# Bias of the values and of the feed-forward output folded into other biases during setup; the first graph's x loaded ahead of the weights

## The reference, cut to what matters

```
q = x @ Wq + bq;  k = x @ Wk + bk          (8 heads of 32)
attn = softmax(q k^T / sqrt(32))
out  = sum over r of (attn * (adj == r)) @ (x @ Wv[r] + bv[r])
x1 = ln(x + out @ Wo + bo) * g1 + beta1
x2 = ln(x1 + gelu(x1 @ W1 + b1) @ W2 + b2) * g2 + beta2
```

## Time and profile before

| | |
|---|---|
| median of 3 runs | 3253.69 us (3249.42 to 3253.93) |
| the profiled execution, its own time | 3253.88 us |
| its span, from first to last instruction | 3252.1 us |
| mean granted clock of TensorE | 0.99 |
| PE busy | 3119.1 us (96%) |
| PE's weight loads, beside the matmuls | 2711.1 us (83%) |
| DVE busy | 2710.2 us (83%) |
| ACT busy | 2063.7 us (63%) |
| POOL busy | 1473.1 us (45%) |

### The profile page before, as it was taken

One profiled execution on the slowest core, in us unless ns is written; L12 is line 12 of the kernel. 1 busy time (PEld: TensorE's weight loads), 2 busy tenths in 40 slices (PEclk: granted clock), 3 DMA queues, 4 the chain that ended last, 5 costly groups with the idle time before them and its releaser, 6 DMA issues.

```text
span 3252.1 us, 77634 instructions
## 1 busy us (share of the span) xinstructions
PE 3119.1 (96%) x28930; PEld 2711.1 (83%) x28930; DVE 2710.2 (83%) x4892; ACT 2063.7 (63%) x4300; POOL 1473.1 (45%) x1549
## 2 busy tenths in 40 slices
PE   3999999999999999999999999999999999999996
PEld 2788888888888888888888888888888888888885
DVE  3688888888888888888888888888888888888884
ACT  2566766766766666666666666666666666666664
POOL 1345345345355355355455454454454454454441
PEclk8999999999999999999999999999999999999997
DMA  4333433433433433433433433433433433433431
GB/s 107 82 80 93 104 78 92 105 78 91 107 78 90 107 78 89 108 78 88 109 78 87 109 79 87 108 79 87 105 82 87 104 84 87 103 85 87 101 84 30
DMA packets 217643, 292.63 MB, mean 90 GB/s; under 512 B 31492, under 2 KB 119048, under 8 KB 217608
## 3 DMA queue, kind: packets, MB, share of 16 engines
q1 hardware_dynamic: 217608, 292.16, 38.0%
HBM read 72.89 MB, written 16.78 MB: 28 GB/s over the span
## 4 chain that ended last, share of the span: by engine, by line
PE 81%; DVE 14%; issue 2%; SPq 1%; DMA 1%; ACT 1%; POOL 0%; DVEq 0%; ACTq 0%; POOLq 0%
PE pair L922 44%; PE pair L952 11%; PE pair L976 7%; DVE n L686 5%; PE pair L1035 4%; PE pair L967 4%; PE pair L968 4%; PE pair L940 3%; PE pair L1044 2%; PE pair L927 2%; DVE n L680 2%; DVE n L744 1%; DVE x2t_lo L659 1%; DVE stats L671 1%; SPq L309 1%
## 5 line engine op out<-in xcount | busy, mean ns | idle before, releaser
L396 POOL TENSOR_TENSOR act_r_lo<-act,act_r_hi 128x512 fp32r<-128x512 f32 x256 | 334.8, 1315 | 748.7 <-DVE act_r_hi L886 550.3
L502 ACT ACTIVATE leaky_s<-leaky_s,low_r 128x256 f32<-128x256 f32 x1024 | 505.9, 498 | 2.9 <-DVE low_r L728 2.1
L523 ACT ACTIVATE probs<-pair 128x1024 f32<-128x1024 f32 x256 | 256.7, 1029 | 202.0 <-PE pair L1044 202.0
L402 POOL TENSOR_TENSOR probs<-probs,rel 128x512 f32<-128x512 f32 x256 | 327.2, 1300 | 124.7 <-ACT probs L523 124.7
L732 DVE TENSOR_REDUCE mx_a<-pair 128x4 f32<-128x1024 f32 x256 | 308.0, 1224 | 80.2 <-PE pair L1035 79.9
L496 ACT ACTIVATE leaky_s<-pair 128x1024 f32<-128x1024 f32 x256 | 261.9, 1023 | 159.3 <-PE pair L968 159.3
L724 DVE TENSOR_TENSOR leaky_s<-pair,leaky_s 128x1024 f32<-128x1024 f32 x256 | 312.1, 1219 | 28.5 <-ACT leaky_s L496 28.3
L728 DVE TENSOR_REDUCE low_r<-leaky_s 128x4 f32<-128x1024 f32 x256 | 310.5, 1213 | 2.2
L492 ACT ACTIVATE probs<-pair 128x1024 f32<-128x1024 f32 x256 | 261.8, 1023 | 63.7 <-PE pair L976 59.5
L402 POOL TENSOR_TENSOR leaky_s<-probs,rel 128x512 f32<-128x512 f32 x256 | 301.9, 1208 | 0.1
L390 POOL TENSOR_TENSOR rstd<-mv,eps 128x2 f32<-128x2 f32 x256 | 68.7, 268 | 482.5 <-DVE mv L675 481.6
(11 more groups left out here) (180 smaller groups left out, 9055.7 us busy)
## 6 DMA issues: line engine op xcount, KB each, us to landing
stack_a<-qk SPq DMA_DIRECT2D x768, 128.0 KB, 2.4
stack_r<-qk SPq DMA_DIRECT2D x768, 128.0 KB, 2.4
xt<-in_xT SPq DMA_DIRECT2D x64, 256.0 KB, 3.9
adj_a<-in_adjT SPq DMA_DIRECT2D x64, 256.0 KB, 3.0
xn<-in_x SPq DMA_DIRECT2D x64, 256.0 KB, 3.8
adj_q<-in_adj SPq DMA_DIRECT2D x64, 256.0 KB, 2.8
out<-n SPq DMA_DIRECT2D x64, 256.0 KB, 2.9
probs<-in_w SPq DMA_DIRECT2D x4, 512.0 KB, 5.2
```

Of the source, the lines that this page charges most:

```text
L396: return nc.gpsimd.tensor_tensor(dst, src, hi, ALU.subtract)
L402: last = nc.gpsimd.tensor_tensor(masked_p[g][:, h], probs[:, g, h], rel1[:], ALU.mult)
L502: last = nc.scalar.activation(leaky_s[:, p % SLOTS, k, t], leaky_s[:, p % SLOTS, k, t], ACT.Exp, bias=low_r[:, p, k, t:t + 1], accum_out=d ...
```

## The change

What it does:
- **Values.** Each row of the attention adds up to 1, so `bv[0]` adds the same row to every node's output, and that row times Wo is a constant: `bo + bv[0] @ Wo`. The setup computes it and puts it in place of `bo`. The first 256 columns of `vee` have no bias now, and its bias matmul is 256 columns wide (for v1 - v0).
- **Feed-forward output.** `b2` is added to `beta1` in the norm's table, so x1 carries it into the residual. So that W1's product stays the same, the setup puts `b1 - b2 @ W1` in place of `b1`. The two bias matmuls of the last `down` are gone.
- **Setup.** PE computes both products from the weights as they were loaded, in float32 (19 matmuls), with one tile of ones and zeros to bring in `b1`. ACT copies the results out. PE's first `body` waits for these copies.
- **Order of the setup.** SP loads x of graph 0 first. Only the constants that the first `body` needs come early; the norms' tables come later. ACT, DVE and SP do their first `body` ahead of the other nine pieces (seven of them on SP), by `turns`'s argument `between`.
- **General path.** It gets a load and four vector operations more.

```diff
-        bias_r = sb("bias_r", [SHIFT, 4 * D], F32R)
-        bv_r, bo_r, b2_r = bias_r[:, 0:2 * D], bias_r[:, 2 * D:3 * D], bias_r[:, 3 * D:]
+        bias_r = sb("bias_r", [SHIFT, 2 * D], F32R)
+        bv_r, bo_r = bias_r[:, 0:D], bias_r[:, D:2 * D]
...
         @block.sync
-            for i, (src, hi, lo) in enumerate(pieces[0:FIRST_W]):
-                sp.dma_start(staged(i, src), src).then_inc(w_loaded[i % STAGES], 16)
-            (all constants, then the other pieces, each with its wait for w_split)
+            def weights(first, last):
+                for i in range(first, last):
+                    if i >= STAGES:
+                        sp.wait_ge(w_split, i - STAGES + 1)
+                    if FOLD_W[0] <= i - STAGES <= FOLD_W[-1]:
+                        sp.wait_ge(f_mm, 1)
+                    src = pieces[i][0]
+                    sp.dma_start(staged(i, src), src).then_inc(w_loaded[i % STAGES], 16)
...
-            turns(sp, body)
+            turns(sp, body, lambda: weights(STAGES + FIRST_W, n_pieces))
...
         @block.scalar
+            def other_weights():
+                weights(FIRST_W, n_pieces)
+                act_e.wait_ge(w_split, n_pieces)
+            weights(0, FIRST_W)
+            act_e.wait_ge(f_loaded, 16 * N_FOLD)
+            nc.scalar.activation(b2_n, b2_c, ACT.Copy, scale=-1.0).then_inc(f_neg, 1)
+            act_e.wait_ge(f_mm, 1)
+            nc.scalar.activation(b1_c, bank(B_X)[:, 0, 0:FT], ACT.Copy).then_inc(f_done, 1)
+            nc.scalar.activation(wo_row, bank(B_X)[0:1, 1], ACT.Copy).then_inc(f_done, 1)
...
         @block.vector
+            def other_weights():
+                dve.wait_ge(late_loaded, 16 * N_LATE)
+                dve.wait_ge(f_done, 2)
+                nc.vector.tensor_tensor(norm[:, E1], norm[:, E1], b2_row, ALU.add).then_inc(bias_done, 1)
+                nc.vector.tensor_tensor(bias_f[:, 2 * D:], bias_f[:, 2 * D:], wo_row, ALU.add).then_inc(bias_done, 1)
+                dve.wait_ge(bias_done, 2)
+                nc.vector.tensor_copy(bias_r[0:1, D:], bias_f[:, 2 * D:]).then_inc(bias_done, 1)
+                dve.wait_ge(bias_done, 3)
+                nc.vector.tensor_tensor(bias_r[32:33, D:], bias_f[:, 2 * D:], bias_r[0:1, D:], ALU.subtract).then_inc(bias_done, 1)
+                weights(FIRST_W, n_pieces)
...
         @block.tensor   (vee, down, setup)
-                products(dst, lambda i, k: parts[i][:, k, t * P:(t + 1) * P], whole(W["wv"]), KT, stop=False)
-                return add_bias(dst, bv_r)
+                products(dst, lambda i, k: parts[i][:, k, t * P:(t + 1) * P], whole(W["wv"]), KT, stop=False, skip=True)
+                return add_bias(dst[:, D:2 * D], bv_r, skip=True)
...
-                                    start=c == 0 and t == 0, stop=False, skip=True)
-                last.then_inc(down_part.sem, 1)
-                if c == NCH - 1:
-                    for t in range(NT):
-                        last = add_bias(bank(B_DN)[:, t], b2_r, skip=True)
-                    last.then_inc(down_mm.sem, 1)
+                                    start=c == 0 and t == 0, stop=c == NCH - 1, skip=True)
+                last.then_inc(down_mm.sem if c == NCH - 1 else down_part.sem, 1)
...
+            for i in FOLD_W:
+                pe.wait_ge(w_loaded[i % STAGES], 16 * (i // STAGES + 1))
+            pe.wait_ge(f_loaded, 16 * N_FOLD)
+            pe.wait_ge(f_neg, 1)
+            wo_f, w1_f = staged(FOLD_W[0], pieces[FOLD_W[0]][0]), [staged(i, pieces[i][0]) for i in FOLD_W[1:]]
+            mm(bank(B_X)[:, 0, 0:FT], ident[:], b1_c, start=True, stop=False, skip_group_check=True)
+            for m in range(FT):
+                for k in range(KT):
+                    mm(bank(B_X)[:, 0, m:m + 1], w1_f[k][:, 0, m * P:(m + 1) * P], b2_n[:, k:k + 1],
+                       start=False, stop=k == KT - 1, skip_group_check=True)
+            for k in range(KT):
+                last = mm(bank(B_X)[0:1, 1], bv0_c[:, k:k + 1], wo_f[:, k], start=k == 0, stop=k == KT - 1, skip_group_check=True)
+            last.then_inc(f_mm, 1)
+            pe.wait_ge(f_done, 2)
             pe.wait_ge(w_split, FIRST_W)
```

More of the change, by code:

```diff
@@ L267, in build @@
         FIRST_W = 2
+        FOLD_W = 2, 3, 4
         n_pieces = len(pieces)
@@ L312, in load @@
             def load(dst, src, graph, form, done):
+                if src is xT and isinstance(graph, int) and graph == 0:
+                    return
                 sp.dma_start(dst[:], src[graph - path.general * G].rearrange(form, p=P)).then_inc(done.sem, 16)
@@ L355, in body @@
                     sp.dma_start(out[g0 - path.general * G].rearrange("(t p) c -> p t c", p=P), result[:]).then_inc(stored.sem, 16)
-            turns(sp, body)
+            def weights(first, last):
[6 more added lines that the diff above has]
+                    sp.dma_start(staged(i, src), src).then_inc(w_loaded[i % STAGES], 16)
+            sp.dma_start(xt[:], xT[0].rearrange("(t p) n -> p t n", p=P)).then_inc(ld_xt.sem, 16)
+            weights(0, FIRST_W)
+            sp.dma_start(v_w[:, 0], v_src[0]).then_inc(c_loaded, 16)
+            sp.dma_start(v_w[:, 1], v_src[1]).then_inc(c_loaded, 16)
+            for k in range(2):
+                sp.dma_start(bias_f[0:1, k * D:(k + 1) * D], w["bv"][k].rearrange("(a c) -> a c", a=1)).then_inc(c_loaded, 16)
+            sp.dma_start(bq_c, w["bq"]).then_inc(c_loaded, 16)
+            sp.dma_start(bk_c, w["bk"]).then_inc(c_loaded, 16)
+            weights(FIRST_W, STAGES)
+            sp.dma_start(bv0_c, w["bv0c"]).then_inc(f_loaded, 16)
+            sp.dma_start(b2_c, w["b2c"]).then_inc(f_loaded, 16)
+            sp.dma_start(b1_c, w["b1"]).then_inc(f_loaded, 16)
+            weights(STAGES, STAGES + FIRST_W)
+            sp.dma_start(bias_f[0:1, 2 * D:], w["bo"].rearrange("(a c) -> a c", a=1)).then_inc(late_loaded, 16)
+            sp.dma_start(b2_row, w["b2"].partition_broadcast(P)).then_inc(late_loaded, 16)
+            for r, row in enumerate(("g1", "e1", "g2", "e2", "lg1", "lb1", "lg2", "lb2")):
+                sp.dma_start(norm[:, r, :], w[row].partition_broadcast(P)).then_inc(late_loaded, 16)
+            turns(sp, body, lambda: weights(STAGES + FIRST_W, n_pieces))
             sp.wait_ge(stored.sem, stored.at(G - 1))
@@ L485, in _, with weights @@
         def _(act_e):
-            for i, (src, hi, lo) in enumerate(pieces):
-                act_e.wait_ge(w_loaded[i % STAGES], 16 * (i // STAGES + 1))
-                nc.scalar.activation(hi, staged(i, src), ACT.Copy).then_inc(w_hi_done, 1)
+            def weights(first, last):
+                for i in range(first, last):
+                    src, hi, lo = pieces[i]
+                    act_e.wait_ge(w_loaded[i % STAGES], 16 * (i // STAGES + 1))
+                    nc.scalar.activation(hi, staged(i, src), ACT.Copy).then_inc(w_hi_done, 1)
+            def other_weights():
+                weights(FIRST_W, n_pieces)
+                act_e.wait_ge(w_split, n_pieces)
+            weights(0, FIRST_W)
+            act_e.wait_ge(f_loaded, 16 * N_FOLD)
[3 more added lines that the diff above has]
+            nc.scalar.activation(wo_row, bank(B_X)[0:1, 1], ACT.Copy).then_inc(f_done, 1)
             def copy(dst, src):
@@ L637, in _, with weights @@
                                   ones[STK:TALL, 0:1].broadcast_to([TALL - STK, H * N])).then_inc(ready, 1)
+            def weights(first, last):
+                for i in range(first, last):
+                    src, hi, lo = pieces[i]
+                    dve.wait_ge(w_hi_done, i + 1)
+                    nc.vector.tensor_tensor(lo, staged(i, src), hi, ALU.subtract).then_inc(w_split, 1)
+            def other_weights():
[8 more added lines that the diff above has]
+                weights(FIRST_W, n_pieces)
             dve.wait_ge(c_loaded, 16 * N_CONST)
@@ L649, in _ @@
                                         W["wv"][0][:, :, r * D:(r + 1) * D], ALU.subtract).then_inc(ready, 1)
-            for i, (src, hi, lo) in enumerate(pieces):
-                dve.wait_ge(w_hi_done, i + 1)
-                nc.vector.tensor_tensor(lo, staged(i, src), hi, ALU.subtract).then_inc(w_split, 1)
+            weights(0, FIRST_W)
             def flat(ap):
```

47 lines of the change are left out of this document (24 added, 23 removed).

## The result

The changed kernel took 3242.57 us (median of 8 runs, 3238.28 to 3248.02), the kernel before 3252.26 beside it (8 runs, 3249.27 to 3254.44): ratio 0.9973, 95% interval 0.9964 to 0.9981. It is faster by 0.27%, 9 us (the medians lie 9.7 us apart). The prediction said 3224 with a range of 3217 to 3230, so the sign was right and two thirds of the gain did not come. The profiled execution took 3238.28 us with a span of 3236.1.

What follows compares the result with a forecast made beforehand. The prediction took PE to bound the kernel, in a cycle of 48.89 us a graph. From 3253.9 us it took 29.2 for the loop and 0.8 for the start-up, giving 3224, range 3217 to 3230.

Steps and rivals of the forecast that it cites:

- The first step, what leaves PE's list: Loop, PE: value biases halve to 256 columns, feed-forward biases go; 0.23 us each a graph, 29.2 us in all.
- the 0.46 forecast: Loop: PE's saving per graph in us, 0.23 from value biases and 0.23 from feed-forward biases.
- is anything next late?: Loop: four places checked for a new wait (DVE's sum, POOL's root, stack copies, stretch before value biases); cost nothing.
- the sum itself: Whole kernel: 3253.9 less 29.2 for the loop and 0.8 for the start-up, said as 3224 us.
- The order of events: Start-up: PE starts graph 0 some 16 us earlier, loads behind stack copies give it back; maxima 59.8 against 60.58.
- the low end of 2.57: Start-up: the last early constant, issued at 4.71, lands after the shortest copy time of 2.57 to 6.12; 7.3.
- The fold: Start-up, PE: 19 float32 matmuls for the new bias constants, taken as 7 us between 2.1 and 11.4.
- Half swallowed: Rival, loop: POOL's root or DVE's order holds the norm, half the loop's gain is lost; 3238.6 us, chance 0.07.
- 512-column matmuls cheap: Rival, loop: a halved bias matmul saves 0.03 us, not 0.11; 0.29 us a graph, 3234.5 us, chance 0.03.
- Start-up loses: Rival, start-up: fold at its upper end and late loads lose 6 us instead of gaining 0.8; 3230.7 us, chance 0.07.
- The stack copies: Rival, loop: fourth score piece waits 1.2 us a graph for its copy; 46 us slower, 3299 us, chance 0.02.
- Its own sign for "wrong": Period above 48.6 us with a new PE wait (x2 or stack_a), or graph 0's maxima done later than 64.

Runs made afterwards that it cites:

- e4: Kernel before with only the loop part of the change (narrower value biases, no feed-forward biases), all addresses kept: 3228.34 us, ratio 0.9917.
- e5: Changed kernel plus 2016 unused bytes, so every tile of the kernel before has its old address: 3230.72 us, ratio 0.9927.
- e3: Kernel before plus an unused 32-byte tile ahead of the norm tables: 3269.17 us, ratio 1.0048.
- e6: e5 with six weight pieces split ahead of graph 0 and loads up to the eleventh piece issued before the stack copies: 3222.21 us, ratio 0.9901.
- e7: Kernel before with 32 unused bytes ahead of the first weight and 32 more behind the last: 3256.21 us, ratio 1.0008.
- e9: Kernel before with 64 unused bytes ahead of the norm tables: 3258.14 us, ratio 1.0018.
- e10: Kernel before with 128 unused bytes ahead of the norm tables: 3249.89 us, ratio 0.9989.
- e12: Kernel before with 64 unused bytes ahead of the two stacks and 64 behind them: 3265.7 us, ratio 1.0037.
- e8: Kernel before with 32 unused bytes ahead of the first weight, so everything moves: 3254.19 us, ratio 1.0005.
- e11: e6 with 64 unused bytes ahead of all weights, so every tile moves by 64: 3207.82 us, ratio 0.9862.

## Why the prediction missed

**Loop.** The first step, what leaves PE's list, was right: biases fell from 1.03 to 0.47 us a graph, and with the 0.09 of idle time that now stands behind the last product in place of the last bias, it is the 0.46 forecast. e4 and e5 give 0.44 and 0.42 a period in all. The question "is anything next late?" was rightly answered with no. The step that failed is the sum itself: it counts the removed instructions alone and puts the change of all other rows at nothing, without a reason and without a word on the smaller `bias_r`. The products of the changed kernel take 26.96 us instead of e5's 26.63, the score pieces 2.11 instead of 2.22. Together that is 0.2 us a graph, or 13 us, lost to addresses that the diff moves without a word. It is 14 of the 18.6 us by which 3224 missed. That is shown in both directions: e3 brings the loss into the kernel before (15.7 us), e5 takes it out of the changed one (14 us). Why these distances cost what they do stays open.

**Start-up.** The order of events was right, and nearly every time in it too early. Constants 8.5 for 7.3: the landing took 4.12 us, not the low end of 2.57. The split of wq ends at 12.9 for 11.8. The half of w1 is used at 16.8 for 16.2. The fold and its two copies took 9.7 us (16.83 to 26.53) for 7.9; PE starts graph 0 at 26.5 for 24.1. k is split at 35.3 for 32.2. From there everything is the forecast plus 3: copies, adj_a, w2's load 43.9 for 40.6, the last split 56.2 for 53.0, scores 57.0 for 53.6, maxima 62.9 for 59.8. The fold was taken at 7 us and took 9.2 (16.83 to 26.03): its one-column matmuls ran as two instructions each, 0.21 us apart, where the sum had 0.11 and 0.30 as its ends. So the mis-sized terms are the fold with its copies (1.8 us), the loads ahead of it (0.6) and graph 0's products up to k (0.7), 3.1 us together, which the range had covered. The medians of e4 and e5, without and with the new start-up, differ by 2.4 us (3 by the ratios), in line with it, though their intervals overlap.

The rest, some 2 us, is the 0.42 to 0.44 of a period in place of 0.46.

**The rivals.** "Half swallowed" gave 3238.6, the number nearest to the result, and its mechanism is not there: DVE's idle time ahead of n did not shrink, PE's wait for n fell, and e5 has the whole gain with the same waits. "512-column matmuls cheap" (3234.5) is refuted by e4. "Start-up loses" was right in kind, 2.3 us of its 6. The stack copies did not become a wait (and that rival's own sum, 3253.9 + 46, gives 3300, not 3299). A number near a rival's is no evidence for it; the rows of its mechanism are.

**The range.** 3217 to 3230 rested on the start-up's steps alone. Its own sign for "wrong", a period above 48.6 with a new wait, came true by half: the period was 48.66, without a new wait.

## To carry to other kernels

When a change resizes, adds or drops a tile, list the start addresses of all tiles before and after, and keep them with an unused tile until the change itself has been timed; then treat the addresses as a knob of their own. On a kernel that PE bounds, a few ns on each of thousands of products outweigh a removed instruction, so compare the mean of every large group, also of those that the diff leaves alone. And where an engine starts earlier, look at once for the queue that everything behind it is issued from: here the gain came only when the loads and splits of the weights were put ahead of the copies (e6).

## What the runs showed of the hardware

- The pace of float32r products hangs on where the two operands lie to each other: 277 ns at the old distance, 281 at 32 bytes more (e3, e7) and at 64 (e9), 280 at 128 more (e10, e12; all for `w_lo,act_r_hi`), unchanged when both move by 32 or 64 (e8, e11). The bfloat16 and transposing matmuls did not change (284 and 272 ns). The rule behind it, and what sets the time of the score pieces (1.97 to 2.25 us a graph), stay open.
- PE's pace at the start has to be read from its rows, not from the view's clock. The view of 27 to 31 us prints 1.00, but the trace's first record of the clock begins at 31.75 us; ahead of it there is none, and the 1.00 there is no measurement. The products of graph 0 stand 0.43 us a pair apart up to 31 us and 0.24 from 32 us on, so their pace doubles where that first record (1.00, the level of 2.4 GHz) begins. In the kernel before it is the same: first record at 43.76 us, products 0.21 us apart until then and 0.12 from 44.8 us on. PE had stood still until 16.83 us here and until 40.04 us there.

```profile
27.00:31.00 4.00, 4.00 (x17) 3.61 (x17) 0.63 (x2) 0.84 (x2) 0.00 (x0) 1.00 0.00 0
```

```profile
27.55 0.63 PE L981 MATMUL pair<-xt_r_hi,wq_lo 128*128 128x256 f32 x2
27.98 0.63 PE L981 MATMUL pair<-xt_r_hi,wq_hi 128*128 128x256 f32 x2
...
32.38 0.40 PE L981 MATMUL pair<-xt_r_hi,wk_lo 128*128 128x256 f32 x2
32.62 0.40 PE L981 MATMUL pair<-xt_r_hi,wk_hi 128*128 128x256 f32 x2
```

- A float32 matmul of one column on a 128x128 stationary tile ran as two instructions that start 0.21 us apart (16 matmuls, 32 instructions, 17.25 to 24.22 us). The load figure of the Trainium skill, "TensorE: Matmul & The Clock Gate" (LDWEIGHTS), 107 ns for 128 columns, is half of it. The fold ran in the stretch without a clock record in which the 256-column products behind it had half their later pace too, and no run has such matmuls at the full one; so what part the clock has in the 0.21 stays open.
